# Third layer: score and mix key tiles in twos, shift products 32 rows deep, maxima of pairs two and three moved

## The reference

```python
Q = (x @ Wq.T).reshape(b, n, H, R)          # x is the normed input, H = 8 heads of R = 64
K = (x @ Wk.T).reshape(b, n, H, R)
V = (x @ Wv.T).reshape(b, n, H, d)
attn = softmax(einsum('bnhr,bmhr->bhnm', Q, K), axis=-1)
out = einsum('bhnm,bmhd->bnd', attn, V)      # summed over the heads
# feed-forward, scale s behind every ternary product
h = silu(x @ w1.T * s1) * (x @ w2.T * s2)
h = gelu(h @ h1.T * sh1); h = gelu(h @ h2.T * sh2); y = h @ w3.T * s3
```

## Time and profile before

| | |
|---|---|
| median of three runs | 1772.31 us |
| the profiled execution, its span | 1771.17 us, 1769.4 us |
| busy: TensorE, VectorE, ScalarE, GpSimd | 94%, 56%, 56%, 42% |
| granted clock, mean | 0.975 of full speed |
| third layer | from about 636 to 1467 us of the span |
| score products L2027, shift L2030, mix L2042, maxima L2003 | 768, 256, 768, 256 products |

### The profile page before, as it was taken

The page is one execution under the profiler, slowest core; times in us unless marked ns, Lnnn a source line. Parts: engine busy times, 40 slices in busy tenths (PEclk is TensorE's granted clock), DMA queues, the critical chain, the costliest instruction groups (busy, mean ns, idle before and its releaser), DMA issues. The chain is left out here.

```text
span 1769.4 us, 21272 instructions
## 1 busy us (share of the span) xinstructions
PE 1657.6 (94%) x7762; PEld 928.3 (52%) x7762; DVE 990.8 (56%) x1580; ACT 988.4 (56%) x1201; POOL 748.2 (42%) x474
## 2 busy tenths in 40 slices
PE   7799999999889999999999999999999987999997
PEld 4232222224446666766667676666667553444443
DVE  4655555553765454544545454544536446888886
ACT  4767777776434535646473655646374653444442
POOL 1000000000653237555574756556474635755563
PEclk8799999999889999999999999999999998999999
DMA  2322222223017600000000000000000001000000
GB/s 80 51 49 49 49 49 49 49 48 127 1 40 187 153 9 1 1 1 1 1 1 1 1 1 1 1 1 1 1 1 1 1 1 51 1 13 6 6 13 12
DMA packets 20550, 49.08 MB, mean 28 GB/s; under 512 B 1056, under 2 KB 1952, under 8 KB 19680
## 3 DMA queue, kind: packets, MB, share of 16 engines
q1 hardware_dynamic: 20448, 47.73, 11.2%
HBM read 45.23 MB, written 2.36 MB: 27 GB/s over the span
## 5 line engine op out<-in xcount | busy, mean ns | idle before, releaser
L1643 POOL TENSOR_TENSOR probs_low<-exped,probs_high 128x1024 fp32r<-128x1024 f32 x128 | 305.2, 2392 | 113.3 <-ACT probs_high L1713 112.9
L527 ACT ACTIVATE probs<-ps 128x1024 f32<-128x1024 f32 x256 | 245.9, 1023 | 88.5 <-PE ps L783 85.6
L1709 ACT ACTIVATE exped<-ps_ring 128x1024 f32<-128x1024 f32 x128 | 131.0, 1023 | 83.8 <-PE ps_ring L2030 82.0
L1809 DVE TENSOR_REDUCE negmax<-ps_o 128x2 f32<-128x1024 f32 x64 | 78.5, 1226 | 126.7 <-PE ps_o L2003 126.7
L1699 ACT ACTIVATE xn<-ps_ring,pack 128x512 f32<-128x512 f32 x64 | 40.6, 684 | 182.1 <-PE ps_ring L1501 182.1
L483 POOL TENSOR_TENSOR sq<-qk 128x1024 f32<-128x1024 f32 x8 | 15.2, 1895 | 292.4 <-DVE qk L565 292.4
L797 PE MATMUL ps<-probs,v 128*32 128x512 f32 x1024 | 137.8, 612 | 0.9 <-DVE o_sb L604 0.9
L1713 ACT ACTIVATE probs_high<-exped 128x1024 fp32r<-128x1024 f32 x128 | 135.7, 1060 | 4.1
L2258 POOL TENSOR_TENSOR rs<-r,state 128x512 f32<-128x512 f32 x64 | 86.4, 1352 | 91.5 <-DVE state L2424 91.5
L1809 DVE TENSOR_REDUCE negmax<-ps_ring 128x2 f32<-128x1024 f32 x64 | 75.4, 1221 | 63.8 <-PE ps_ring L2003 63.7
L2424 DVE TENSOR_TENSOR_SCAN state<-decay,state,kv 128x511 f32<-128x511 f32 x64 | 99.1, 1548 | 6.9 <-issue 1.6
(11 more groups left out here) (432 smaller groups left out, 3797.8 us busy)
## 6 DMA issues: line engine op xcount, KB each, us to landing
cwb<-combine_by_expert SPq DMA_DIRECT2D x8, 2048.0 KB
score<-score_by_expert SPq DMA_DIRECT2D x15, 1024.0 KB, 8.0
pack<-pack_dram SPq DMA_DIRECT2D x1, 3328.0 KB, 13.9
x<-x_in SPq DMA_DIRECT2D x2, 1024.0 KB, 6.1
out<-x SPq DMA_DIRECT2D x8, 256.0 KB, 2.0
pack<-pack_dram SPq DMA_DIRECT2D x1, 1992.0 KB, 7.6
pack<-pack_dram SPq DMA_DIRECT2D x1, 1543.0 KB, 6.4
pack<-pack_dram SPq DMA_DIRECT2D x1, 1140.0 KB, 9.4
```

Of the source, the lines that this page charges most:

```text
L527: nc.scalar.activation(probs[n % 3][:, 2 * half:2 * half + 2, :], ps, ACT.Exp, scale=float(HD0) ** -0.5).then_inc(read, 1)
L1643: nc.gpsimd.tensor_tensor(single(probs_low[:, m, :, :]), exped[:, n % EXPED2, :, :], probs_high[:, m, :, :], ALU.subtract).then_inc(low_re ...
L1709: nc.scalar.activation(exped[:, n % EXPED2, :, :], ps, ACT.Exp).then_inc(read, 1)
L1809: nc.vector.reduce_max(negmax[:, n % 2, :, m], ps[:, :, :], AX_X, negate=True).then_inc(read, 1)
```

## The change

Key tiles are mixed and scored in twos (`mix_two`, `scores_of_two`): first the products with high parts of both tiles, which wait for the high parts alone, then those with low parts. Both score tiles are filled, then one shift product per tile and head, 32 rows deep, each on another quarter of the array's rows; the DMAs bring the shift to four rows (0, 32, 64, 96) in place of two. ScalarE does two exponents and then two high parts. Maxima of pair 2 move between the feed-forward's products, which now hold twelve in place of eight, and those of pair 3 to the first three halves; `ps_o` serves three pairs' maxima, and `negmax` has a place for every pair, in columns of a weight that was used up at the start. The turn of pair 1 moves into h2's second half. The 16 positions become 8 halves; both projections of a pair stand in the half after the next.

```diff
 # the ring's order list, behind the first half of h1
-        order += [..., ("h2", b, 0), ("turn", b, 0), ("h2", b, 1), ("score", b, 0, 0), ("score", b, 0, 1),
-                  ("y", b), ("score", b, 0, 2), ("score", b, 0, 3), ("turn", b, 1)]
+        order += [..., ("h2", b, 0), ("turn", b, 0), ("h2", b, 1), ("turn", b, 1), ("score", b, 0, 0), ("score", b, 0, 1),
+                  ("y", b), ("score", b, 0, 2), ("score", b, 0, 3)]
...
+            def shift_product(ps, n, j, a):
+                group = slice(64 * j + 32 * a, 64 * j + 32 * a + 32)
+                return nc.tensor.matmul(ps[:, j, :], single(ones_row[group, :]), single(sh_row[n % 2][group, :]), start=False, stop=True)
+            def scores_of_two(b, p, m):
+                if m == 0:
+                    shift_rows_loaded(b, p)
+                two = []
+                for a in range(2):
+                    two.append(empty(pe, ("score", b, p, m + a)))
+                    score_products(two[a][0], p, m + a)
+                for a, (ps, done) in enumerate(two):
+                    for j in range(2):
+                        last = shift_product(ps, b * PAIRS + p, j, a)
+                    last.then_inc(done, 1)
+            def mix_two(b, p, first):
...
+                for m in range(first, first + 2):
+                    pe.wait_ge(high_ready, b * HIGHS2 + 5 + p * NBLK + m + 1)
+                    average_of(m, xt_low, probs_high, m == 0, False)
+                    average_of(m, xt_high, probs_high, False, False)
+                for m in range(first, first + 2):
+                    pe.wait_ge(low_ready, low_count(b, p, m))
+                    last = average_of(m, xt_high, probs_low, False, m == NBLK - 1)
+                last.then_inc(values_done, 1)
...
 # TensorE's list, feed-forward part and pairs
+                hide1(b, 0, nothing, lambda: maxima(b, 0, 0), lambda: maxima(b, 0, 1))
+                maxima(b, 0, 2)
+                if b:
+                    turn_attention(b - 1)
+                hide1(b, 1, lambda: maxima(b, 0, 3), lambda: maxima(b, 1, 0), lambda: maxima(b, 1, 1))
+                maxima(b, 1, 2)
+                hide2(b, 0, lambda: turn_max(b, 0), lambda: maxima(b, 1, 3), lambda: maxima(b, 2, 0))
+                maxima(b, 2, 1)
+                hide2(b, 1, lambda: turn_max(b, 1), lambda: maxima(b, 2, 2), lambda: maxima(b, 2, 3))
+                scores_of_two(b, 0, 0)
+                down(b)
+                scores_of_two(b, 0, 2)
+                for half in range(2 * PAIRS):
+                    p, m = half // 2, half % 2 * 2
+                    mix_two(b, p, m)
+                    if half == 2:
+                        maxima(b, 3, 3)
+                    if half == 1:
+                        turn_max(b, 2)
+                        maxima(b, 3, 1)
+                    if half == 3:
+                        turn_max(b, 3)
+                    if half == 5 and b + 1 < B:
+                        average(b + 1, "var", sq[:, :])
+                    if p + 1 < PAIRS:
+                        scores_of_two(b, p + 1, m)
+                    if half < 2:
+                        maxima(b, 3, 2 * half)
+                    if p and m == 0:
+                        project_mixed(b, p - 1, 0)
+                    if half == 2 and b + 1 < B:
+                        average(b + 1, "mean", x[:, at(b + 1)])
+                    if p and m == 0:
+                        project_mixed(b, p - 1, 1)
+                    if b == B - 1:
+                        if half:
+                            spread_mean3(half - 1)
+                        if half < B - 1:
+                            mean3(half)
...
 # ScalarE's list
+                    if b == B - 1 and half:
+                        square3(half - 1)
+                    if m:
+                        take_mixed(b, p)
+                    if p + 1 < PAIRS:
+                        probabilities_of_two(b, p + 1, m)
+                    if half == 5 and b + 1 < B:
+                        rstd(b + 1)
+                    if b == B - 1 and half:
+                        root3(half - 1)
```

More of the change, by code:

```diff
@@ L1467, in ring_order2 @@
             order.append(("att", b - 1))
-        order += [("h1", b, 1), ("h2", b, 0), ("turn", b, 0), ("h2", b, 1), ("score", b, 0, 0), ("score", b, 0, 1),
-                  ("y", b), ("score", b, 0, 2), ("score", b, 0, 3), ("turn", b, 1)]
[L1470 to L1483, removed]
+        order += [("h1", b, 1), ("h2", b, 0), ("turn", b, 0), ("h2", b, 1), ("turn", b, 1), ("score", b, 0, 0), ("score", b, 0, 1),
+                  ("y", b), ("score", b, 0, 2), ("score", b, 0, 3)]
+        for half in range(2 * PAIRS):
+            p, m = half // 2, half % 2 * 2
+            if half == 2:
+                order.append(("max", b, 3, 3))
+            if half == 1:
+                order += [("turn", b, 2), ("max", b, 3, 1)]
+            if half == 3:
+                order.append(("turn", b, 3))
+            if half == 5 and b + 1 < B:
+                order.append(("var", b + 1))
+            if p + 1 < PAIRS:
+                order += [("score", b, p + 1, m), ("score", b, p + 1, m + 1)]
+            if half < 2:
+                order.append(("max", b, 3, 2 * half))
+            if p and m == 0:
+                order.append(("out", b, p - 1, 0))
+            if half == 2 and b + 1 < B:
+                order.append(("mean", b + 1))
+            if p and m == 0:
+                order.append(("out", b, p - 1, 1))
+            if b == B - 1:
+                order += [("var3", half - 1)] * (half > 0) + [("mean3", half)] * (half < B - 1)
     return order + [("out", B - 1, PAIRS - 1, 0), ("out", B - 1, PAIRS - 1, 1), ("att", B - 1)]
@@ L1490, in top_order2 @@
     for b in range(B):
-        order += [("max", b, p, m) for p in range(2) for m in range(NBLK)]
+        order += [("max", b, p, m) for p in range(3) for m in range(NBLK)]
         order += [("mixed", b, p) for p in range(PAIRS)]
@@ L1737, in _ @@
                 nc.scalar.preload_act_table_set("natural_log_exp_and_others")
[L1738 to L1749, removed]
+                probabilities_of_two(b, 0, 0)
+                probabilities_of_two(b, 0, 2)
+                for half in range(2 * PAIRS):
+                    p, m = half // 2, half % 2 * 2
+                    if half == 4 and b + 1 < B:
+                        square(b + 1)
+                    if b == B - 1 and half:
[8 more added lines that the diff above has]
+                        root3(half - 1)
         @block.vector
@@ L1804, in maximum @@
             def maximum(b, p, m):
[L1805 to L1809, removed]
+                ps, read = top_filled(dve, ("max", b, p, m)) if p < 3 else filled(dve, ("max", b, p, m))
+                if m == 0 and b:
+                    filled(dve, ("turn", b - 1, p))
+                nc.vector.reduce_max(negmax[:, p, :, m], ps[:, :, :], AX_X, negate=True).then_inc(read, 1)
             def take_rows(b, p):
@@ L1873, in _ @@
                 maximum(b, 0, 1)
+                maximum(b, 0, 2)
                 split_hidden(b, "h1", 0)
@@ L1885, in _ @@
+                maximum(b, 2, 2)
+                maximum(b, 2, 3)
                 split_hidden(b, "h2", 1)
-                maximum(b, 1, 3)
                 add_hidden(b)
[L1888 to L1905, removed]
+                for half in range(2 * PAIRS):
+                    p, m = half // 2, half % 2 * 2
+                    if half == 2:
+                        maximum(b, 3, 3)
+                    if half == 1:
+                        take_rows(b, 2)
+                        maximum(b, 3, 1)
+                    if half == 3:
+                        take_rows(b, 3)
+                    if half < 2:
+                        maximum(b, 3, 2 * half)
+                    if half == 6 and b + 1 < B:
+                        normed(b + 1)
+                    if p and m == 0:
+                        normalise(b, p - 1, 0)
+                    if half == 2 and b + 1 < B:
+                        centre(b + 1)
+                    if p and m == 0:
+                        normalise(b, p - 1, 1)
+                    if b == B - 1:
+                        if half:
+                            scale3(half - 1)
+                        if half < B - 1:
+                            centre3(half)
@@ L1955, in turn_x, with hide1 @@
                 last.then_inc(done, 1)
-            def hide1(b, i, between):
+            def hide1(b, i, *between):
                 ps, done = empty(pe, ("h1", b, i))
@@ L2028, in scores @@
                                          start=(i == 0), stop=False)
[L2029 to L2034, removed]
-                if m == 0:
+            def shift_product(ps, n, j, a):
+                group = slice(64 * j + 32 * a, 64 * j + 32 * a + 32)
+                return nc.tensor.matmul(ps[:, j, :], single(ones_row[group, :]), single(sh_row[n % 2][group, :]), start=False, stop=True)
+            def scores_of_two(b, p, m):
```

(21 more changed lines are left out.)

90 lines of the change are left out of this document (52 added, 38 removed).

## The result

The changed kernel takes 1787.26 us (median of five runs, 1780.85 to 1790.04) against 1772.03: ratio 1.008, 95% interval 1.0058 to 1.0102. In a second set, eleven runs gave 1787.31, ratio 1.0062 (1.0042 to 1.0083). Two executions, 8764.86 us of the kernel before and 4300.33 us of turn_late, stand out as slow and are left out of the ratios and spreads. The forecast was 1788. The kernel is slower, as forecast, but only 9.7 of the +16 forecast for the third layer are found there, as the stages show.

What follows compares the result with a forecast made beforehand. TensorE's instruction stream was taken as the bound. Per batch -0.2 work, -2.1 waits going, +5.5 coming, rounded to +3.0; seven batches +21, last -5, so +16 on 1771.2: 1787, median 1788 us, range 1760 to 1800.

Steps and rivals of the forecast that it cites:

- Work: TensorE's own work per batch: twos -2.5, lone maxima +2.0, shift products +0.3; sum -0.2 us.
- Step from 64 to 32 rows: Before each shift group: costs like 128 to 64, so group 0.44 against 0.46 us; with two maxima behind groups, +0.3 a batch.
- the free step: Rival: the step into shift groups costs nothing, work 2.1 us lower a batch; total 1774, no change; chance 0.18.
- Waits that go: Per batch: shift rows' DMA -1.2, ring tile -0.7, ahead of the down product -0.2; together -2.1 us.
- Waits that come: Five new TensorE waits per batch for ring tiles and ScalarE, GpSimd and VectorE results, with a VectorE queue delay; +5.5 us.
- head: Start of the pairs' part: TensorE has 7.5 us of work against 8.2 until the last low part; +0.7 us a batch.
- mean and second projections: Mean and second projections of pairs 0 and 1 take tiles of scores just issued, read by exponents; +0.9 us a batch.
- end: Batch end: 7.7 us of work against 9.6 needed by the next batch, +1.9; inside it a 2.1 projection wait behind rstd.
- Last batch: Its pairs' part: squares' waits of 4.1 us and twice 1.3 of clock loss go, 3.0 of ring waits stay; -5 us.
- the one in which the shift products run one after the other: Rival: a shift group takes 0.9 us instead of 0.44; +30 us, up to 1818; chance 0.05.
- The clock did not drop at the new ends: Rival judged here: waits of 2.1 us at batch ends lower the clock, +9 us, total 1797; chance 0.12.
- the new waits bind: Forecast's claim; its rival: ScalarE and GpSimd keep up, waits 3 to 5 vanish; 1761 us, 1745 with free step; chance 0.18.

Runs made afterwards that it cites:

- turn_late: The changed kernel with the turn of pair one's maxima, and its ring tile, moved behind the down product; 1771.10 us, ratio 0.9983 to the kernel before.
- shift64: The changed kernel with shift products 64 rows deep again, two pairs in place of one group of four; 1773.50 us, ratio 1.0007 to the kernel before.
- rstd_first: The changed kernel with rstd on ScalarE ahead of the exponents of pair three's last two tiles; 1775.41 us, ratio 1.0017 to the kernel before.
- after_again: The changed kernel run again with no edit; 1787.31 us, ratio 1.0062 to the kernel before.
- ones_turn: The kernel before, with pair one's maxima one place earlier and their turn inside the down product; 1764.11 us, ratio 0.9928 to the kernel before.

## Why the prediction was right, and where it was not

The sign and the mechanism held. Step by step, per batch:

- *How a wait is measured.* The lists count a wait from the recorded end of the product before. Products 0.23 us apart last 0.39 in the records, so most waits delay the stream by 0.1 to 0.2 more than listed. "By starts" below is the distance from start to start less what the same two shapes take where nothing waits, in one batch; it is an estimate.
- *Work.* Predicted -0.2. Busy time is 3.8 more in the feed-forward part, 3.2 of it the price of five more lone maxima (0.63 each, as predicted: 0.32 ahead and 0.77 behind, less two slots), and 2.6 less in the pairs' part: +1.2, by records that overlap. What the waits by starts leave of the measured +2.50 a batch is +0.3 to +0.4, an estimate.
- *Step from 64 to 32 rows.* I took the upper bound, and it was exact (0.33 and 0.44). The chance of 0.18 for the free step was too high after a trace in which no step was free. The Trainium skill (TensorEngine Tiling (Array Packing), Tiling Modes) says that changing the tiling mode drains TensorE. The trace agrees in that this step delays the products too; whether a drain is the reason it does not show.
- *Waits that go.* Predicted 2.1. The DMA's, the ring's and the one ahead of the down product are off the list, 2.3 by starts. The gates' wait for VectorE (0.6 listed, 0.8 by starts) went too, which I had not foreseen: it is hidden behind the one for low_x. Together 3.1.
- *Waits that come.* Predicted, and measured by starts (listed): score tile (0,1) 1.2, 1.15 (0.97); turn of pair one 0.65, 0.69 (0.53); a maximum behind VectorE's queue 0.15, none over 0.1; head 0.7, 0.49 (0.33); mean and second projections 0.9, about 0.5 (too short to be listed); end 1.9, 1.52 for rstd's tile (1.56) and 0.68 for low_x (0.51). With a delay of 0.17 at a product of L1509, not foreseen, that is 5.2 or so against the predicted 5.5.
- *Seven batches.* +21 predicted, 7 x 2.50 = +17.5 measured: the waits that go were the term most out of size, 2.1 for 3.1. (The check sum of the pairs' part adds to 58.4, not 58.5, which changes nothing.)
- *Last batch.* -5 predicted, 108.1 - 115.9 = -7.8 measured. The waits for the squares fell from 4.1 to 0.6 and the clock stayed at 1.00. Of the 3.0 that I kept for ring tiles, because averages take tiles of scores just issued, the list shows 1.4 behind exponents, 0.7 at each of two places. Third layer: +16 predicted, +9.7 measured.
- *The total.* That 1787.26 fell within 1 us of the forecast is luck. The sum behind 1788 was 6 too high for the third layer; something else made up for it. Part of that is the clock that an execution draws: at a mean granted clock of 0.974 and more, the medians of the two kernels are 1780.87 and 1770.94 (7 and 19 executions), 9.9 apart, near the 9.7; at 0.970 to 0.971 they are 1787.47 and 1775.12 (5 and 8), 12.4 apart. The changed kernel does not draw worse clocks (mean 0.972 in both), but its median falls among the later of its executions: six lie at 1779.7 to 1782.8, ten at 1784.6 to 1792.6. The single edits too gain more in total, by medians, than in the third layer (shift64 13.8 and 8.6, rstd_first 11.9 and 5.9, turn_late 16.2 and 12.3). Where those 4 to 6 us lie stays open.

Of the rivals, the free step is out (shift64 and the timeline). So is the one in which the shift products run one after the other: the four start within 0.01 us of each other. The clock did not drop at the new ends (1.00 in both parts of a batch). That the new waits bind was shown by turn_late and rstd_first, which removed them and gained.

## What to carry to other kernels

Where one engine's stream is the bound and buffers form a ring, write down for every use who reads the tile of the use it follows: one turn moved in that list, with the copy that reads it, was worth 12 us here. Here work put alone between products of another shape paid for the step twice, and beside its like for its slot only (0.63 against 0.23 us). Count a concurrent group together with the step into its shape: four products in one slot gained nothing here and cost 8.6 us through what they delayed.

## What the runs showed of the hardware that I had not expected

The granted clock ahead of the third layer differs between executions of the same code. The same 35 us of both kernels, before and changed (busy us and count of PE, PEld, DVE, ACT, POOL; clock):
```profile
430.00:465.00 35.00, 30.71 (x193) 18.94 (x192) 20.12 (x36) 19.88 (x51) 15.56 (x16) 0.90 0.31 132
```
```profile
430.00:465.00 35.00, 32.82 (x122) 21.45 (x121) 16.37 (x31) 17.12 (x44) 7.54 (x7) 0.61 0.35 150
```
The two counts are not of the same products, since the executions come to different points. The same 193 products or so, from the last of L1063 (start 430.09 and 431.59) to the first of L1046 (464.87 and 473.42), took 34.8 us at a mean clock of 0.90 in the kernel before and 41.8 at 0.67 in the changed one, so that 7 of the 8.6 us of the late start come from here. They took 41.8 at 0.67 in after_again too, 38.6 at 0.82 in turn_late and 43.4 at 0.72 in ones_turn. Why the clock differs between executions no run shows.

A copy on VectorE took 2.46 us in all seven batches of the changed kernel, each time beside a low part on GpSimd, where the same copy took 0.43 with GpSimd idle beside it, in the kernel before and in rstd_first. VectorE and GpSimd in the changed kernel's timeline:
```profile
1048.07 5.15 POOL L1651 TENSOR_TENSOR probs_low<-exped,probs_high 128x1024 fp32r<-128x1024 f32 x2 [3.26 <-ACT probs_high L1724]
...
1051.04 2.46 DVE L1786 CAST xh<-xn 128x512 fp32r<-128x512 f32 x1
...
1053.59 1.28 POOL L1630 TENSOR_TENSOR xl<-xn,xh 128x512 fp32r<-128x512 f32 x1 [0.36 <-DVE xh L1786]
```
The copy starts in the second low part, which ends at 1053.22, and itself ends 0.28 later, at 1053.50; low_x could start only then. That the copy is held until GpSimd is through fits this, but no run tested it alone.
